# Weight tensors of an FFN copied once to bf16 in HBM, their loads moved to the Sync queue, and a preparation step moved within its slot

## The chip, the cores and the metric

The kernel runs on all 8 cores of one Trainium2 chip. Each core works on its own 2048 tokens, with its own copy of the weights, and no core talks to another. The metric is the device time of the slowest core in microseconds (us). The median of 3 runs of the kernel before is 6087.93 us.

## What is computed

One "sandwich" block on x of shape (4, 4096, 2048), f32 (`_layernorm` has no gain or bias):

```python
def attn(x, Wqkv, bqkv, Wout, bout):          # C=32 groups of K=64
    xc = x.reshape(N, Ls, 32, 64)
    qkv = einsum('nlck,cki->nlci', xc, Wqkv) + bqkv
    q, k, v = split(qkv, 3, axis=-1)
    scores = einsum('nlcd,nled->nldce', q, k) / 8
    attn = softmax(scores, axis=-1)
    ctx = einsum('nldcm,nlcd->nldm', attn, v).transpose(0, 1, 3, 2)
    return einsum('nlck,ko->nlco', ctx, Wout) + bout

def ffn(x, w_gate, w_up, w_down):              # 2048 -> 8192 -> 2048
    gated = silu(x @ w_gate.T) * (x @ w_up.T)
    return gated @ w_down.T

x = x + layernorm(attn(layernorm(x)))
x = x + layernorm(ffn(layernorm(x)))
```

The attention is within one token, between its 32 groups; it is done by elementwise work, not by matmuls. The FFN is the matmul work.

## The kernel before

Features lie on the partitions, tokens on the free axis. **Chunks**: a core's 2048 tokens are 16 chunks of T = 128 tokens for the attention. **Windows**: 4 windows of W = 512 tokens (4 chunks each) for the FFN. The three FFN weights (`wgH`, `wuH`, `wdH`, each 8192 x 2048 in f32, 67 MB) do not fit on the chip, so they are streamed from HBM once for each window, 768 loads in all, and each load casts a block of 128 x 2048 from f32 to bf16 on its way. Such a cast DMA is issued from GpSimd (POOL).

**Slots.** The main loop (L570) runs c from -1 to 16; one turn is a slot. Slot c does: the end of the attention of chunk c-1 (output projection L612, LayerNorm, residual, the new x2, L651, its statistics, and the store of x2 to the HBM scratch `x2h`, "spill", L677, from Sync); if chunk c-1 was the last of its window, `emit_xn2prep` (L528), which reads x2 of the whole window back in 16 DMAs on Sync and normalizes it into `xn2_sb` in 32 vector instructions (L558, L561); the load `dma_xb(c+2)` (L161); the input statistics of chunk c+1 (ACT L694, PE L171); then the attention loop of chunk c, 17 steps j; then `xn1` and QKV of chunk c+1 (L239, L273).

**A step j** (L758): `emit_s(j)`, the score product on the vector engine (L716, 128 x 4096); `emit_z(j-1)`, a tree sum (L725 to L735); `emit_rz` on ACT (L742, L745); `emit_uP(j-1)`, (L302, L311, L320); one `pull(1)`; `emit_exp(j)` on ACT (L753, 3.6 us); another `pull(1)`.

**Atoms.** `pull` emits the next atom of the FFN of the window before: per window 32 `gu` atoms, 16 `down`, 32 `gu`, 16 `down`, `ln4`, `bc4` and 16 `fin`, 114 in all, split over the four slots of the next window at 29 a slot. So slots 0 to 3 have no FFN atoms, slot 4 has 29 `gu` atoms, slots 4 to 15 carry windows 0 to 2, and slot 16 carries window 3 alone. What is left of a slot's atoms after the loop is emitted at its end (after QKV).

- `gu(h)` (L327): loads `wg_sb[h%2]` and `wu_sb[h%2]`, 16 matmuls 128x512 for gate (L341), 16 for up (L351), then three ACT and two vector instructions for silu and product into `gated_sb`.
- `down(hh, dt)` (L384): two halves; each loads `wd_sb[half]` (L391) and runs 16 matmuls (L402) into `dps[dt%2]`. The evacuation is on ACT for hh = 0 (L414) and on the vector engine for hh = 1 (L418).
- `fin(k)` (L496): reads x2 back (`x2s_sb`, Sync), three vector instructions, stores `yT` (Sync).

**Order.** `plan.op` appends to one list per engine ("T" PE, "V" vector, "A" ACT, "G" POOL, "S" Sync), and each engine works its list in the order of emission; a wait of one entry holds all that follow on that engine. A weight load is emitted just before its matmuls and waits only until PE has finished with its buffer two loads earlier. On the POOL list stand `wqkv`, `wout`, three `xb` loads at the start, and then, in order, `xb` and weight loads; `dma_xb(c+2)` waits for the x2 of chunk c-1.

Of the kernel before, what the change touches and what calls it, by code (L numbers as in the profile page):

```python
# [6 lines left out]
BF16 = mybir.dt.bfloat16  # L7
# [4 lines left out]
D = 2048  # L12
HID = 8192
# [38 lines left out]
def build_program(max_slot=NC):  # L52
# [9 lines left out]
    bk_d = nc.dram_tensor("bk", [128, 32], F32, kind="ExternalInput").ap()  # L62
    bv_d = nc.dram_tensor("bv", [128, 16], F32, kind="ExternalInput").ap()
    bo_d = nc.dram_tensor("bo", [128, 1], F32, kind="ExternalInput").ap()
    x2h = nc.dram_tensor("x2h", [D, TOK], BF16, kind="ExternalOutput" if DBG_X2 else "Internal").ap()
    yT = nc.dram_tensor("yT", [D, TOK], F32, kind="ExternalOutput").ap()

# [63 lines left out]
    def dep(*keys):  # L131
        return [last.get(k) for k in keys]
# [24 lines left out]
    def dma_xb(c):  # L157
        buf = xb_sb[c % 3]

        def fn(g, c=c, buf=buf):  # L160
            return g.dma_start(out=buf.ap(),  # L161
                               in_=xH[c * 128:(c + 1) * 128, :])
        last[f"xb{c}"] = plan.op("G", fn, deps=dep(f"x2_{c - 3}"),
                                 inc=f"Dxb{c % 3}")
# [162 lines left out]
    def emit_gu(w, h):  # L327
        pb = h % 2
        def d_g(g, h=h, pb=pb):
            return g.dma_start(out=wg_sb[pb].ap(),  # L330
                               in_=wgT[h * 128:(h + 1) * 128, :])
        tg = plan.op("G", d_g, deps=dep(f"wgfree{pb}"), inc=f"Dwg{pb}")
        def d_u(g, h=h, pb=pb):
            return g.dma_start(out=wu_sb[pb].ap(),
                               in_=wuT[h * 128:(h + 1) * 128, :])
        tu_d = plan.op("G", d_u, deps=dep(f"wufree{pb}"), inc=f"Dwu{pb}")
        first = [tg, last[f"xn2_{w}"]] + dep(f"gufree{pb}")
        tk = None
        for ft in range(NFT):
            def fn(tn, ft=ft, pb=pb):  # L340
                return tn.matmul(out=gps[pb].ap(),  # L341
                                 lhsT=wg_sb[pb].ap()[:, ft * 128:(ft + 1) * 128],
                                 rhs=xn2_sb.ap()[:, ft * W:(ft + 1) * W],
                                 start=(ft == 0), stop=(ft == NFT - 1))
            tk = plan.op("T", fn, deps=first if ft == 0 else (),
                         inc="T" if ft == NFT - 1 else None)
        tgate = tk
        last[f"wgfree{pb}"] = tgate
        for ft in range(NFT):
            def fn(tn, ft=ft, pb=pb):  # L350
                return tn.matmul(out=ups[pb].ap(),  # L351
                                 lhsT=wu_sb[pb].ap()[:, ft * 128:(ft + 1) * 128],
                                 rhs=xn2_sb.ap()[:, ft * W:(ft + 1) * W],
                                 start=(ft == 0), stop=(ft == NFT - 1))
            tk = plan.op("T", fn, deps=[tu_d] if ft == 0 else (),
                         inc="T" if ft == NFT - 1 else None)
        tup = tk
        last[f"wufree{pb}"] = tup
        if h == NHT - 1:
            last["xn2_free"] = tup  # L360
        ta = plan.op("A", lambda a, pb=pb: a.activation(  # L361
            out=e1_sb.ap(), in_=gps[pb].ap(), func=AF.Exp, scale=-1.0),
            deps=[tgate] + dep("e1free"), inc="A")
        ta = plan.op("A", lambda a: a.activation(
            out=e1_sb.ap(), in_=e1_sb.ap(), func=AF.Ln, bias=1.0),
            deps=[ta] + dep("consts"), inc="A")
        ta = plan.op("A", lambda a, pb=pb: a.activation(  # L367
            out=m_sb[pb].ap(), in_=e1_sb.ap(), func=AF.Exp, scale=-1.0),
            deps=[ta] + dep(f"mfree{pb}"), inc="A")
        last["e1free"] = ta  # L370
        tv = plan.op("V", lambda v, pb=pb: v.tensor_mul(  # L371
            out=t1_sb[pb].ap(), in0=m_sb[pb].ap(), in1=gps[pb].ap()),
            deps=[ta, tgate] + dep(f"t1free{pb}"), inc="V")
        last[f"mfree{pb}"] = tv
        hs = h % 32
        tv = plan.op("V", lambda v, hs=hs, pb=pb: v.tensor_mul(  # L376
            out=gated_sb.ap()[:, hs * W:(hs + 1) * W],
            in0=t1_sb[pb].ap(), in1=ups[pb].ap()),
            deps=[tup, tv] + dep(f"gatedfree{hs}"), inc="V")
        last[f"t1free{pb}"] = tv  # L380
        last[f"gufree{pb}"] = tv
        last[f"gated{hs}"] = tv

    def emit_down(w, hh, dt):  # L384
        pb = dt % 2
        tk = None
        for half in (0, 1):
            wb = (2 * dt + half) % 2
            def d_w(g, hh=hh, dt=dt, half=half, wb=wb):
                r0 = (((2 * hh + half) * 16 + dt)) * 128  # L390
                return g.dma_start(out=wd_sb[wb].ap(),  # L391
                                   in_=wdT[r0:r0 + 128, :])
            td = plan.op("G", d_w, deps=dep(f"wdfree{wb}"),
                         inc=f"Dwd{wb}")
            first = [td]
            if half == 0:
                first += [last.get(f"dfree{pb}")] + \
                    [last[f"gated{i}"] for i in range(32)]
            for sh in range(16):
                ht = 16 * half + sh  # L400
                def fn(tn, ht=ht, sh=sh, pb=pb, wb=wb, half=half):
                    return tn.matmul(  # L402
                        out=dps[pb].ap(),
                        lhsT=wd_sb[wb].ap()[:, sh * 128:(sh + 1) * 128],
                        rhs=gated_sb.ap()[:, ht * W:(ht + 1) * W],
                        start=(ht == 0), stop=(ht == 31))
                tk = plan.op("T", fn, deps=first if sh == 0 else (),
                             inc="T" if (sh == 15) else None)
            last[f"wdfree{wb}"] = tk
# [156 lines left out]
    dma_xb(0)  # L566
    dma_xb(1)
    dma_xb(2)

    for c in range(-1, min(max_slot, NC) + 1):  # L570
        pw = (c // CPW) - 1 if 0 <= c < NC else (NW - 1 if c == NC else -1)
# [109 lines left out]
            if cp % CPW == CPW - 1:  # L681
                last[f"spill_w{cp // CPW}"] = ts

        if 0 <= c - 1 < NC and (c - 1) % CPW == CPW - 1:
            emit_xn2prep((c - 1) // CPW)

        if 3 <= c + 2 < NC:
            dma_xb(c + 2)
# [14 lines left out]
        if 0 <= c < NC:  # L703
# [47 lines left out]
            def emit_exp(j):  # L751
# [3 lines left out]
                    deps=[last[f"s_{c}_{j}"]], inc="A")  # L755
                last[f"exp_{c}_{j}"] = ta

            for j in range(NJ + 1):  # L758
                if j < NJ:
                    emit_s(j)  # L760
                if j >= 1:
                    emit_z(j - 1)
                    emit_rz(j - 1)
                if j >= 1:
                    emit_uP(c, j - 1)
                pull(1)
                if j < NJ:
                    emit_exp(j)
                pull(1)

        if 0 <= c + 1 < NC:
            cn = c + 1
# [16 lines left out]
            if "qkv" not in DBG_SKIP:  # L789
# [6 lines left out]

    sems = {name: nc.alloc_semaphore(f"s{name}") for name in plan.counts}

    qsems = {"G": ("Dcq", "Dco", "Dxb0", "Dxb1", "Dxb2",
                   "Dwg0", "Dwg1", "Dwu0", "Dwu1", "Dwd0", "Dwd1"),  # L800
             "S": ("Db", "Dxw", "Dr0", "Dr1", "Do",
                   "Dxr0", "Dxr1", "Dxr2", "Dxr3")}

    def run_stream(eng_handle, name):
        hw = {k: 0 for k in sems}
# [134 lines left out]
```

How the kernel before makes its waits and increments, by code:

```python
    def run_stream(eng_handle, name):  # L804
        hw = {k: 0 for k in sems}
        for fn, waits, inc in plan.ops[name]:
            for s, v in waits:
                if v > hw[s]:
                    eng_handle.wait_ge(sems[s], v)
                    hw[s] = v
            inst = fn(eng_handle)
            if inc is not None:
                inst.then_inc(sems[inc], 16 if inc.startswith("D") else 1)
        for s in qsems.get(name, ()):
            v = plan.counts.get(s, 0)
            if v > hw.get(s, 0):
                eng_handle.wait_ge(sems[s], v)
                hw[s] = v
        return hw
# [18 lines left out]
        @block.sync  # L838
        def _(sync):
            hw = run_stream(sync, "S")
            if out_final and hw.get("Do", 0) < out_final:
                sync.wait_ge(sems["Do"], out_final)
```

## Time and profile before

| what | value |
|---|---|
| timed runs | 6038.36, 6087.93, 6142.63 us; median 6087.93 us |
| the profiled execution | 5889.32 us; span of its slowest core 5887.8 us |
| spans of the 8 cores | 5833.5 to 5887.8 us, granted TensorE clock 0.775 to 0.782 |
| busy share of the span: PE, vector (DVE), ACT, POOL | 56%, 55%, 35%, 7% |
| HBM read, written by the core | 843 MB, 25 MB |
| cast queue (POOL's DMAs) | 413 MB written on chip, 42.4% of the 16 DMA engines' time |
| chain that ended last, by engine | PE 38%, DVE 25%, DMA 15%, issue 11%, ACT 10% |
| the same by line, the first | gate matmuls 13%, up matmuls 12%, load of `wd_sb` 11%, down matmuls 10% |

The profile is of one execution, of the core that took longest. Its times count from the first instruction. "Busy" of PE counts matmuls as modelled; the granted clock is the share of full speed that PE was allowed. A releaser ("<-") is what ended an engine's idle time. The span is some 0.05% shorter than the execution's own time, and the execution is 3.3% shorter than the median of the timed runs.

### The profile page before, as it was taken

To read this page: it belongs to the slowest core of one execution; us is meant where nothing else is said; L and a number is where in the kernel's file an instruction comes from. 1 tells how busy PE (TensorE), PEld (TensorE's weight loads), DVE (VectorE), ACT (ScalarE), POOL (GpSimd) and SP (SyncE) were. 2 spreads that over 40 slices of the span, in tenths; PEclk is the share of its full clock that TensorE was granted. 3 is DMA by queue.
4 is the path that set the end of the run, shared out by engine and by line. 5 is a ranking of instruction groups with operands and counts; after the bars stand their busy time and mean duration, and the time that the engine had idled before them with its cause. 6 is when DMAs were issued, how large, how long until landed. Compare 5 with 4: busy or idle time off the path is not lost.

```text
span 5887.8 us, 47487 instructions; the slowest of 8 cores (5833.5 to 5887.8 us)
## 1 busy us (share of the span) xinstructions
PE 3298.7 (56%) x15536; PEld 1508.5 (26%) x15536; DVE 3220.9 (55%) x3680; ACT 2043.1 (35%) x2953; POOL 415.7 (7%) x790
## 2 busy tenths in 40 slices
PE   1101102967787511967878521867868521988973
PEld 0101001432343201433333201333333200433431
DVE  5686775754656465764656455765557456100102
ACT  3434433442453323452343323452343322211200
POOL 0000000100010000100101000101101000111100
PEclk9955555979889755878978765988979765999996
DMA  1000002845565312745656311745746321977852
GB/s 26 8 0 7 0 7 42 138 73 95 97 116 99 69 32 49 129 73 96 110 95 113 63 41 45 127 75 101 129 73 114 61 55 43 152 118 120 153 100 67
DMA packets 174676, 458.26 MB, mean 78 GB/s; under 512 B 49376, under 2 KB 65760, under 8 KB 174304
## 3 DMA queue, kind: packets, MB, share of 16 engines
q0 software_dynamic: 113184, 413.22, 42.4%
q1 hardware_dynamic: 61248, 41.99, 2.6%
q8 instruction: 128, 2.10, 0.1%
q14 instruction: 116, 0.95, 0.1%
HBM read 843.15 MB, written 25.17 MB: 147 GB/s over the span
## 4 chain that ended last, share of the span: by engine, by line
PE 38%; DVE 25%; DMA 15%; issue 11%; ACT 10%; DVEq 1%; SPq 0%; ACTq 0%; POOL 0%; POOLq 0%
PE gps L341 13%; PE ups L351 12%; DMA wd_sb<-wdH 11%; PE dps L402 10%; DVE es_sb L311 6%; DVE zs_sb L731 4%; DVE ctx_sb L320 3%; DVE zs_sb L725 3%; DVE es_sb L716 3%; ACT kd_sb L252 2%; DMA x2s_sb<-x2h 2%; PE mps L179 1%; ACT v_sb L289 1%; DMA xn_sb<-x2h 1%; ACT q_sb L289 1%
## 5 line engine op out<-in xcount | busy, mean ns | idle before, releaser
L402 PE MATMUL dps<-gated_sb,wd_sb 128*128 128x512 bf16 x4096 | 1011.4, 408 | 376.2 <-DMA wd_sb<-wdH 343.3
L341 PE MATMUL gps<-xn_sb,wg_sb 128*128 128x512 bf16 x4096 | 981.3, 395 | 55.8 <-DVE gated_sb L376 39.7
L351 PE MATMUL ups<-xn_sb,wu_sb 128*128 128x512 bf16 x4096 | 957.5, 388 | 0.0
L753 ACT ACTIVATE es_sb<-es_sb 128x4096 bf16<-128x4096 bf16 x256 | 922.0, 3602 | 11.4 <-DVE es_sb L716 11.4
L239 PE MATMUL mps<-xn_sb,wqkv_sb 128*128 128x128 bf16 x512 | 72.4, 302 | 1426.6 <-DVE xn_sb L784 1375.1
L742 ACT ACTIVATE rz_sb<-zf_sb 128x128 bf16<-128x128 bf16 x256 | 79.0, 308 | 1977.3 <-DVE zf_sb L735 1977.3
L402 PEld LDWEIGHTS dps<-gated_sb,wd_sb 128*128 128x128 bf16 x4096 | 412.0, 103 | 974.9 <-issue 592.0
L311 DVE TENSOR_TENSOR es_sb<-es_sb,u_sb 128x4096 bf16<-128x4096 bf16 x256 | 586.8, 2292 | 27.7 <-DVE u_sb L302 1.4
L716 DVE TENSOR_TENSOR es_sb<-q_sb,kd_sb 128x4096 bf16<-128x4096 bf16 x256 | 584.7, 2285 | 8.7 <-DVE ctx_sb L316 0.5
L371 DVE TENSOR_TENSOR t_sb<-m_sb,gps 128x512 bf16<-128x512 bf16 x256 | 175.2, 685 | 719.4 <-ACT m_sb L367 718.3
L320 DVE TENSOR_TENSOR ctx_sb<-ctx_sb,es_sb 128x4096 bf16<-128x4096 bf16 x240 | 550.0, 2292 | 26.0 <-DVE es_sb L311 1.4
L341 PEld LDWEIGHTS gps<-xn_sb,wg_sb 128*128 128x128 bf16 x4096 | 409.9, 101 | 590.7 <-issue 215.1
L351 PEld LDWEIGHTS ups<-xn_sb,wu_sb 128*128 128x128 bf16 x4096 | 408.1, 100 | 507.4 <-issue 102.0
L239 PEld LDWEIGHTS mps<-xn_sb,wqkv_sb 128*128 128x128 bf16 x512 | 45.9, 129 | 1456.6 <-issue 1456.6
L731 DVE TENSOR_TENSOR zs_sb<-zs_sb 128x1024 bf16<-128x1024 bf16 (+2 forms) x768 | 360.8, 470 | 81.3 <-DVE zs_sb L731 1.8
L725 DVE TENSOR_TENSOR zs_sb<-es_sb 128x2048 bf16<-128x2048 bf16 x256 | 311.9, 1218 | 134.4 <-ACT es_sb L753 134.4
L192 DVE TENSOR_SCALAR st_sb<-mps 1x128 f32<-1x128 f32 x48 | 13.4, 279 | 518.6 <-PE mps L179 518.6
L361 ACT ACTIVATE e_sb<-gps 128x512 f32<-128x512 f32 x256 | 149.7, 585 | 382.2 <-PE gps L341 382.2
L418 DVE TENSOR_TENSOR y_sb<-y_sb,dps 128x512 bf16<-128x512 bf16 x64 | 43.8, 685 | 376.9 <-PE dps L402 376.7
L302 DVE TENSOR_TENSOR u_sb<-v_sb,rz_sb 128x128 bf16<-128x128 bf16 x256 | 57.7, 225 | 324.2 <-ACT rz_sb L745 324.2
L414 ACT ACTIVATE y_sb<-dps 128x512 bf16<-128x512 f32 x64 | 38.2, 597 | 560.6 <-PE dps L402 560.6
L391 POOL DMA_DIRECT2D wd_sb<-wdH x256 | 135.7, 531 | 1349.4 <-PE dps L402 1303.8
(84 smaller groups left out, 2376.0 us busy)
## 6 DMA issues: line engine op xcount, KB each, us to landing
wg_sb<-wgH POOLq DMA_DIRECT2D x256, 512.0 KB, 6.5
wu_sb<-wuH POOLq DMA_DIRECT2D x256, 512.0 KB, 6.6
wd_sb<-wdH POOLq DMA_DIRECT2D x256, 512.0 KB, 5.5
yT<-outs_sb SPq DMA_DIRECT2D x64, 256.0 KB, 2.5
xb_sb<-xH POOLq DMA_DIRECT2D x16, 512.0 KB, 9.1
x2h<-x2c_sb SPq DMA_DIRECT2D x16, 512.0 KB, 4.3
xn_sb<-x2h SPq DMA_DIRECT2D x64, 128.0 KB, 2.7
x2s_sb<-x2h SPq DMA_DIRECT2D x64, 128.0 KB, 3.4
```

Source lines behind the costliest of these rows:

```text
L311: tp = plan.op("V", lambda v, s3=s3, ub=ub: v.tensor_tensor(out=s3, in0=s3, in1=ub, op=ALU.mult), deps=[tu], inc="V")
L320: tg = plan.op(eng, lambda g, buf=buf: g.tensor_add(out=ctx_sb.ap(), in0=ctx_sb.ap(), in1=buf.ap()), deps=[tp, last[f"ctxadd_{c}_{j - 1}"] ...
L341: return tn.matmul(out=gps[pb].ap(), lhsT=wg_sb[pb].ap()[:, ft * 128:(ft + 1) * 128], rhs=xn2_sb.ap()[:, ft * W:(ft + 1) * W], start=(ft = ...
L351: return tn.matmul(out=ups[pb].ap(), lhsT=wu_sb[pb].ap()[:, ft * 128:(ft + 1) * 128], rhs=xn2_sb.ap()[:, ft * W:(ft + 1) * W], start=(ft = ...
L361: ta = plan.op("A", lambda a, pb=pb: a.activation(out=e1_sb.ap(), in_=gps[pb].ap(), func=AF.Exp, scale=-1.0), deps=[tgate] + dep("e1free") ...
L371: tv = plan.op("V", lambda v, pb=pb: v.tensor_mul(out=t1_sb[pb].ap(), in0=m_sb[pb].ap(), in1=gps[pb].ap()), deps=[ta, tgate] + dep(f"t1fre ...
L391: return g.dma_start(out=wd_sb[wb].ap(), in_=wdT[r0:r0 + 128, :])
L402: return tn.matmul(out=dps[pb].ap(), lhsT=wd_sb[wb].ap()[:, sh * 128:(sh + 1) * 128], rhs=gated_sb.ap()[:, ht * W:(ht + 1) * W], start=(ht ...
L716: v.tensor_tensor(out=s3, in0=qb, in1=k3, op=ALU.mult), deps=d, inc="V")
L725: tz = plan.op("V", lambda v, buf=buf: v.tensor_add(out=zs_sb.ap(), in0=buf.ap()[:, 0:16 * T], in1=buf.ap()[:, 16 * T:32 * T]), deps=[last ...
L731: tz = plan.op("V", lambda v, ww=ww: v.tensor_add(out=zs_sb.ap()[:, 0:ww], in0=zs_sb.ap()[:, 0:ww], in1=zs_sb.ap()[:, ww:2 * ww]), deps=[t ...
L753: ta = plan.op("A", lambda a, buf=buf: a.activation(out=buf.ap(), in_=buf.ap(), func=AF.Exp, scale=0.125), deps=[last[f"s_{c}_{j}"]], inc="A")
```

## The change

Three HBM tensors `wgc`, `wuc`, `wdc` in bf16 are added. At the start, after the three `xb` loads, twelve DMAs on POOL copy and cast the weights into them, in quarters of 2048 rows, in the order g0, u0, d0, g1, u1, d1, and so on. All 768 weight loads of the atoms now read the bf16 copies, are issued from Sync instead of POOL, and wait for the quarter they read (`wcg`, `wcu`, `wcd`) besides their buffer. So `dma_xb(3)` and later ones follow the twelve copies on POOL, and the weight loads share Sync's list with spills, read-backs and `yT` stores.

In slots 4, 8 and 12 `emit_xn2prep` is emitted after step j = 4 of the attention loop instead of before the loop, and in every first slot of a window `pull` is called only from j = 5 on. In slot 16 it stays where it was.

```diff
--- before.py
+++ after.py
@@ -62,6 +62,9 @@
     bk_d = nc.dram_tensor("bk", [128, 32], F32, kind="ExternalInput").ap()
     bv_d = nc.dram_tensor("bv", [128, 16], F32, kind="ExternalInput").ap()
     bo_d = nc.dram_tensor("bo", [128, 1], F32, kind="ExternalInput").ap()
+    wgc = nc.dram_tensor("wgc", [HID, D], BF16, kind="Internal").ap()
+    wuc = nc.dram_tensor("wuc", [HID, D], BF16, kind="Internal").ap()
+    wdc = nc.dram_tensor("wdc", [HID, D], BF16, kind="Internal").ap()
     x2h = nc.dram_tensor("x2h", [D, TOK], BF16, kind="ExternalOutput" if DBG_X2 else "Internal").ap()
     yT = nc.dram_tensor("yT", [D, TOK], F32, kind="ExternalOutput").ap()
 
@@ -328,12 +331,14 @@
         pb = h % 2
         def d_g(g, h=h, pb=pb):
             return g.dma_start(out=wg_sb[pb].ap(),
-                               in_=wgT[h * 128:(h + 1) * 128, :])
-        tg = plan.op("G", d_g, deps=dep(f"wgfree{pb}"), inc=f"Dwg{pb}")
+                               in_=wgc[h * 128:(h + 1) * 128, :])
+        tg = plan.op("S", d_g, deps=dep(f"wgfree{pb}", f"wcg{h // 16}"),
+                     inc=f"Dwg{pb}")
         def d_u(g, h=h, pb=pb):
             return g.dma_start(out=wu_sb[pb].ap(),
-                               in_=wuT[h * 128:(h + 1) * 128, :])
-        tu_d = plan.op("G", d_u, deps=dep(f"wufree{pb}"), inc=f"Dwu{pb}")
+                               in_=wuc[h * 128:(h + 1) * 128, :])
+        tu_d = plan.op("S", d_u, deps=dep(f"wufree{pb}", f"wcu{h // 16}"),
+                       inc=f"Dwu{pb}")
         first = [tg, last[f"xn2_{w}"]] + dep(f"gufree{pb}")
         tk = None
         for ft in range(NFT):
@@ -389,8 +394,9 @@
             def d_w(g, hh=hh, dt=dt, half=half, wb=wb):
                 r0 = (((2 * hh + half) * 16 + dt)) * 128
                 return g.dma_start(out=wd_sb[wb].ap(),
-                                   in_=wdT[r0:r0 + 128, :])
-            td = plan.op("G", d_w, deps=dep(f"wdfree{wb}"),
+                                   in_=wdc[r0:r0 + 128, :])
+            td = plan.op("S", d_w,
+                         deps=dep(f"wdfree{wb}", f"wcd{2 * hh + half}"),
                          inc=f"Dwd{wb}")
             first = [td]
             if half == 0:
@@ -566,6 +572,13 @@
     dma_xb(0)
     dma_xb(1)
     dma_xb(2)
+    for s in range(4):
+        for name_, dst_, src_ in (("g", wgc, wgT), ("u", wuc, wuT),
+                                  ("d", wdc, wdT)):
+            def fcache(g, dst_=dst_, src_=src_, s=s):
+                return g.dma_start(out=dst_[s * 2048:(s + 1) * 2048, :],
+                                   in_=src_[s * 2048:(s + 1) * 2048, :])
+            last[f"wc{name_}{s}"] = plan.op("G", fcache, inc=f"Dwc{name_}{s}")
 
     for c in range(-1, min(max_slot, NC) + 1):
         pw = (c // CPW) - 1 if 0 <= c < NC else (NW - 1 if c == NC else -1)
@@ -681,8 +694,11 @@
             if cp % CPW == CPW - 1:
                 last[f"spill_w{cp // CPW}"] = ts
 
-        if 0 <= c - 1 < NC and (c - 1) % CPW == CPW - 1:
-            emit_xn2prep((c - 1) // CPW)
+        def xn2prep_if_due():
+            if 0 <= c - 1 < NC and (c - 1) % CPW == CPW - 1:
+                emit_xn2prep((c - 1) // CPW)
+        if not (0 <= c < NC):
+            xn2prep_if_due()
 
         if 3 <= c + 2 < NC:
             dma_xb(c + 2)
@@ -755,6 +771,7 @@
                     deps=[last[f"s_{c}_{j}"]], inc="A")
                 last[f"exp_{c}_{j}"] = ta
 
+            jp0 = 5 if c % CPW == 0 else 0
             for j in range(NJ + 1):
                 if j < NJ:
                     emit_s(j)
@@ -763,10 +780,14 @@
                     emit_rz(j - 1)
                 if j >= 1:
                     emit_uP(c, j - 1)
-                pull(1)
+                if j >= jp0:
+                    pull(1)
                 if j < NJ:
                     emit_exp(j)
-                pull(1)
+                if j >= jp0:
+                    pull(1)
+                if j == 4:
+                    xn2prep_if_due()
 
         if 0 <= c + 1 < NC:
             cn = c + 1
@@ -796,10 +817,11 @@
 
     sems = {name: nc.alloc_semaphore(f"s{name}") for name in plan.counts}
 
-    qsems = {"G": ("Dcq", "Dco", "Dxb0", "Dxb1", "Dxb2",
-                   "Dwg0", "Dwg1", "Dwu0", "Dwu1", "Dwd0", "Dwd1"),
+    qsems = {"G": tuple(["Dcq", "Dco", "Dxb0", "Dxb1", "Dxb2"]
+                        + [f"Dwc{n}{s}" for n in "gud" for s in range(4)]),
              "S": ("Db", "Dxw", "Dr0", "Dr1", "Do",
-                   "Dxr0", "Dxr1", "Dxr2", "Dxr3")}
+                   "Dxr0", "Dxr1", "Dxr2", "Dxr3",
+                   "Dwg0", "Dwg1", "Dwu0", "Dwu1", "Dwd0", "Dwd1")}
 
     def run_stream(eng_handle, name):
         hw = {k: 0 for k in sems}
```

## Rows read from the trace of the kernel before

**Rows 1.** The page, 40 slices of 147 us: busy tenths of PE.

```profile
PE   1101102967787511967878521867868521988973
```

**Rows 2.** Groups by line: count, busy us, mean ns, idle us before, what ended it.

```profile
L402 PE MATMUL dps<-gated_sb,wd_sb 128*128 128x512 bf16 x4096 | 1011.4, 408 | 376.2 <-DMA wd_sb<-wdH 343.3 <-DVE gated_sb L376 28.2 <-DVE ctx_sb L320 2.2
L341 PE MATMUL gps<-xn_sb,wg_sb 128*128 128x512 bf16 x4096 | 981.3, 395 | 55.8 <-DVE gated_sb L376 39.7 <-DVE xn_sb L561 15.0 <-DMA wg_sb<-wgH 1.0
```

**Rows 3.** Timeline in the down stretch of slot 5: start us, duration, engine, line.

```profile
1470.24 0.53 POOL L391 DMA_DIRECT2D wd_sb<-wdH  x1 [3.58 <-PE dps L402]
...
1471.77 3.61 PE L402 MATMUL dps<-gated_sb,wd_sb 128*128 128x512 bf16 x16 [2.07 <-DMA wd_sb<-wdH]
...
1480.02 0.53 POOL L391 DMA_DIRECT2D wd_sb<-wdH  x1 [3.57 <-PE dps L402]
```

**Rows 4.** Windows: length, busy us (count) per engine, clock, DMA share, GB/s.

```profile
1312.00:1658.00 346.00, 240.38 (x1122) 108.43 (x1122) 185.40 (x201) 124.98 (x182) 31.15 (x59) 0.86 0.55 92
1340.00:1510.00 170.00, 120.66 (x511) 50.00 (x512) 82.38 (x76) 40.62 (x39) 17.94 (x34) 0.95 0.57 98
...
5015.00:5218.00 203.00, 201.99 (x937) 91.43 (x936) 41.13 (x60) 53.82 (x87) 30.08 (x57) 1.00 0.97 150
5218.00:5391.00 173.00, 124.55 (x513) 50.77 (x512) 0.00 (x0) 9.24 (x16) 17.95 (x34) 0.93 0.59 99
5391.00:5612.00 221.00, 220.63 (x1023) 99.81 (x1020) 43.50 (x64) 59.71 (x97) 32.71 (x62) 1.00 0.88 151
```

**Rows 5.** Timeline, vector engine: the score product, once per step j, three places.

```profile
595.95 2.29 DVE L716 TENSOR_TENSOR es_sb<-q_sb,kd_sb 128x4096 bf16<-128x4096 bf16 x1
...
607.45 2.29 DVE L716 TENSOR_TENSOR es_sb<-q_sb,kd_sb 128x4096 bf16<-128x4096 bf16 x1
...
1110.15 2.28 DVE L716 TENSOR_TENSOR es_sb<-q_sb,kd_sb 128x4096 bf16<-128x4096 bf16 x1
...
1125.35 2.28 DVE L716 TENSOR_TENSOR es_sb<-q_sb,kd_sb 128x4096 bf16<-128x4096 bf16 x1
...
1425.23 2.29 DVE L716 TENSOR_TENSOR es_sb<-q_sb,kd_sb 128x4096 bf16<-128x4096 bf16 x1
...
1445.58 2.29 DVE L716 TENSOR_TENSOR es_sb<-q_sb,kd_sb 128x4096 bf16<-128x4096 bf16 x1
```

**Rows 6.** The page's DMA issues: line, queue, count, KB each, median us to landing.

```profile
wd_sb<-wdH POOLq DMA_DIRECT2D x256, 512.0 KB, 5.5
yT<-outs_sb SPq DMA_DIRECT2D x64, 256.0 KB, 2.5
...
x2h<-x2c_sb SPq DMA_DIRECT2D x16, 512.0 KB, 4.3
...
wqkv_sb<-wqkv POOLq DMA_DIRECT2D x1, 2048.0 KB, 18.8
```

**Rows 7.** The page's DMA queues: packets, MB, share of 16 engines' span.

```profile
q0 software_dynamic: 113184, 413.22, 42.4%
```

**Rows 8.** Timeline at the start of slot 2.

```profile
511.93 0.37 SPq L677 DMA_DIRECT2D x2h<-x2c_sb  x1
...
512.40 0.53 POOL L161 DMA_DIRECT2D xb_sb<-xH  x1 [231.47 <-DVE x2c_sb L651]
...
515.57 1.06 PE L171 MATMUL mps<-xb_sb,ones_c 128*1 128x128 bf16 x16
...
524.11 4.47 DVE L716 TENSOR_TENSOR es_sb<-q_sb,kd_sb 128x4096 bf16<-128x4096 bf16 x2
```

**Rows 9.** DMA issues of the first 60 us.

```profile
xb_sb<-xH POOLq DMA_DIRECT2D x3, 512.0 KB, 23.9
```

**Rows 10.** Timeline at the start of slot 4.

```profile
977.09 0.53 POOL L161 DMA_DIRECT2D xb_sb<-xH  x1 [232.54 <-DVE x2c_sb L651]
...
1001.31 0.42 DVE L558 TENSOR_TENSOR xn_sb<-xn_sb,a2bc_sb 128x512 bf16<-128x512 bf16 x1 [1.13 <-DMA xn_sb<-x2h]
...
1015.03 2.27 DVE L716 TENSOR_TENSOR es_sb<-q_sb,kd_sb 128x4096 bf16<-128x4096 bf16 x1
```

## The prediction

> **What bounds the kernel now.** I read the page's slices first [rows 1]. Up to slice 6 PE is nearly idle: slots 0 to 3 have attention and no FFN work. Then FFN and attention share the core (slots 4 to 15), and the last six slices or so are FFN alone. Next the groups by line [rows 2], for what ended PE's idle time: it stood 343.3 us before L402, the down matmuls, for `wd_sb`, while the gate matmuls waited 1.0 us for their weights (39.7 us went to `gated_sb`). So two buffers suffice for gate and up, and not for down.
>
> The windows and the timeline show how. At 1470 us [rows 3] a half of a down atom needs 3.61 us of PE and has waited 2.07 us; its load is issued when PE has read the buffer two halves back, and lands some 5.5 us later [rows 6]. Issue to issue of one buffer is 1470.24 to 1480.02, 9.8 us for the two halves of one `dt`. PE could do them in 7.2 us. A down `dt` took 170/16 = 10.6 us in slot 5 and 173/16 = 10.8 us in the last window [rows 4]. The granted clock of these stretches (0.93 to 0.95, a mean of both levels) is below the 1.00 of the gate/up stretch at 5391 us, where PE never waits: the gaps cost clock also.
>
> Elsewhere PE is not the limit. One step j of a slot takes 11.5 us without FFN work (595.95 to 607.45 us), 15.2 us with two gate/up atoms, and 20 to 21 us with two down atoms of the first half [rows 5]. In the first two the vector engine sets the pace; in the third it waits, in the end for PE. Only the third can shrink by faster loads, and its floor is two atoms of PE, 14.4 us.
>
> **The change, part by part.**
>
> *(a) Faster down loads: gain.* All 768 weight loads move to SP and read bf16, half the bytes. No load of this kind is in the trace. The old one takes 5.5 us. The mean packet of the cast queue took 0.424 x 5887.8 x 16 / 113184 = 0.353 us, eight per DMA engine and load, so 2.8 us is transfer and 2.7 us is fixed; with half the bytes read I estimate 1.4 us plus a fixed part as SP's rows have it. Bounds on SP: 256 KB in 2 KB rows lands in 2.5 us, 512 KB in small pieces in 4.3 us [rows 6, 7]. I take 3.4 us, since 4 KB rows resemble the first more. Now 9.8 us is 5.5 us of landing and 4.3 us of PE and handover; SP also starts sooner, since after the same vector instruction SP issued at 511.93 and POOL at 512.40 [rows 8], 0.4 to 0.5 us. That makes 3.4 + 4.3 - 0.4 = 7.3 us per `dt`; with some slow clock 7.5. Gain: 96 `dt` in slots x (10.7 - 7.5) = 307 us (10.7 for the slots where down and other atoms alternate) and 32 at the end x (10.8 - 7.5) = 106 us, together about 410 us. At 4.3 us landing a `dt` costs 8.2 to 8.6 us and the gain is some 290 us; at PE's own pace (7.2 us) it is 336 + 115 = 451 us. Gate and up loads waited for nothing and bring nothing.
>
> *(b) The caches: cost.* Twelve DMAs on POOL read 12 x 16.8 = 201 MB as f32 and write 101 MB as bf16, HBM to HBM. They stand in the queue behind `wqkv` and the first three `xb` loads (landed by about 28 us) [rows 9] and **ahead of `dma_xb(3)`**. All of the cast DMAs of the trace ran on one queue, q0 [rows 7], so I expect `xb3` to come only after the last cache byte. What waits: at slot 2's start PE's L171 reads `xb3` at 515.57, and ACT's L694 soon after [rows 8]. Both engines take work in order; behind them stand the exp of the softmax and, through the statistics, the vector engine's first L716. Nothing covers this: slots 0 to 3 have no FFN work. The stall is (end of the cache + some 7 us for `xb3`) - 516 us. The end:
> - quickest: 24576 rows of 4 KB at the mean packet time, 24576 x 0.353 / 16 = 542 us, end at 570, stall 61 us;
> - at the pace of the `wqkv` load, the only large one (2048 KB written, 4.19 MB read, 18.8 us [rows 6]): 201.3 / 4.19 x 18.8 = 903 us, end at 931, stall 422 us;
> - slowest: in 5015 to 5218 us the core wrote 150 GB/s into SBUF, so read 300 GB/s from HBM, with the DMA engines 0.97 busy, against 0.88 for the same rate at 5391 us [rows 4]: memory already slows packets. If that is the limit for reads and writes together, 302 MB take 1007 us, stall 526 us.
>
> I take 421 us. The quickest would need 302 / 542 = 557 GB/s of HBM traffic per core, nearly twice anything in the trace, so the truth is nearer to the other two.
>
> The Trainium skill ("HBM Reference", Specifications) gives about 716 GB/s per stack, shared by the two cores on it. By that figure, an estimate, the caches take 2 x 302 MB / 716 GB/s = 843 us and the stall is about 362 us; no run so far shows HBM-to-HBM traffic.
>
> The first cached weights are needed in slot 4 (1015 us before, later now), so the SP waits on `wcg0` and the others are over by then, even in the slowest case with its stall.
>
> *(c) `xn2` preparation moved behind j = 4 in slots 4, 8, 12: about nothing.* Before, the vector engine waits at the boundary to slot 4 for the read-backs of x2. From the issue of the `xb` load to the slot's first L716 it is 11.7 us in slot 2 (512.40 to 524.11) [rows 8] and 37.9 us in slot 4 (977.09 to 1015.03) [rows 10], so 26 us are exposed. After: the reads land during steps 0 to 4; the vector work stays, 32 x 0.42 us [rows 10] = 13.4 us. So 12.6 us are saved. But steps 0 to 4 have no atoms, the remaining 12 steps hold 24, and five of the 29 gate/up atoms come after QKV with the vector engine all but idle: 5 x 6.9 (221 us for 32 atoms) [rows 4] = 35 us. Against this, a step with two atoms costs 3.7 us more than one without: 14.5 such steps before, 12 after, so 9 us less. Sum per window: -12.6 + 35 - 9 = +13; where the five atoms overlap ACT's evacuations it is less: I take +7 us each, +20 in all, bounds 0 and +50.
>
> *(d) SP's queue.* Weight loads now stand behind the spill (waits for x2), the read-backs and the `yT` stores (wait for the vector engine). Before, they stood behind `dma_xb(c+2)`, which waits for the same x2 [rows 8]; in fin phases no weights are wanted. Nothing. Where a weight load was late at a slot start (all gate matmuls together waited 1.0 us) [rows 2], nothing either.
>
> **Sum** against the profiled span: 5887.8 - 410 + 421 + 20 = 5919 us, 0.5% up. The profiled execution took 5889.32 us and the timed runs 6087.93 us in the median, 3.4% more. Scaled: 6088 x 1.0053 = 6120 us. In slower executions PE is slower, so (a) may give less there.
>
> **Rivals.**
> 1. *The caches run at the DMA engines' pace* (stall 61 us). For: the packet time of the queue as a mean. Against: the traffic it needs. Span 5887.8 - 410 + 61 + 20 = 5559 us, about 5748 us. A `xb3` that overtakes the caches would end near there as well (another 60 us less). It decides from a stall under about 270 us, caches done by 780 us.
> 2. *Other side: HBM takes reads and writes at 300 GB/s per core together* (stall 526 us). Span 6024 us, 2.3% up, about 6229 us. For: the busy share of 0.97. Against: that rate was what PE asked for, not proven a ceiling. It decides from a stall of about 510 us, that is caches ending after 1020 us.
> 3. *SP's loads land in 4.3 us*: gain 290 us, span 6039 us, about 6244 us. For: the only 512 KB row on SP. Against: its pieces are small.
> 4. *The clock*: once waits are gone, PE may be granted no more than the mean 0.86 of slot 5 [rows 4]; a `dt` then costs 7.2 / 0.86 = 8.4 us, the gain is 96 x 2.3 + 32 x 2.4 = 298 us, the span 6031 us, about 6236 us.
>
> **Chances.** My forecast (stall 300 to 510, gain near 410): 0.50. Rival 1 with overtaking: 0.19. Rival 2: 0.16. Rivals 3 and 4: 0.15. The forecast's own range is 6000 to 6215 us. A comparison of this kernel can tell about 2% (122 us) from no change: faster 0.20 (rival 1 and the forecast's lower edge), same 0.50, slower 0.30 (rivals 2 to 4, nearly whole). Range for 8 in 10: it leaves out rival 1 (0.19), reaches to 6260 us for rivals 2 to 4, and 5960 us below, a stall of some 265 us.
>
> **What would show it.** The vector and PE slices should be empty from about 516 to 930 us, with ACT's L694 waiting for `xb_sb` near 420 us, and DMA full from 28 us on. `PE dps L402 <- DMA wd_sb` should fall from 343 us to under 60 us, `wd_sb` land in about 3.4 us from SP, and steps with two down atoms take 15 us. Slot 4 should lose its wait for `xn_sb<-x2h` and show five gate/up atoms behind QKV. I am wrong if `xb3` lands before 800 us, or if down steps stay above 17 us.

## The result, and the profile after

The changed kernel takes 6002.4 us in the median of its runs, the kernel before 6022.25 us over all runs made beside it. The ratio is **1.0119, 95% interval 1.0083 to 1.0155**: by 2% no difference, but reliably above 1. Executions in which one die had a lower granted clock are in the medians and not in the ratio, which is why the two stand in another order. I forecast 1.0053 (6120 us, range 5960 to 6260) and 0.50 for "same". The two profiled spans are 5887.8 and 5989.8 us, +102 us. The ratio is worth only some 70 us: the profiled execution of the kernel before (5889 us) was quicker than all ten timed beside the changed one (5909 us at best), so differences of spans against 5888 us, here and below, are up to some 30 us too large.

The page of the changed kernel: busy tenths in 40 slices of 150 us, the rate of the DMA engines, and the two queues.

```profile
PE   1101000101979686315886866039796960399993
...
DVE  5681004686846585668556664768365856520112
...
DMA  9999994001434232112332422114242320244442
GB/s 116 109 109 109 109 109 51 7 0 35 135 91 148 77 127 78 48 36 100 113 120 92 131 81 74 39 56 139 90 151 74 127 75 31 85 151 144 150 136 79
...
q1 hardware_dynamic: 171840, 444.69, 22.8%
q0 software_dynamic: 5856, 111.18, 16.6%
```

Against [rows 1] there is a hole: PE and the vector engine are all but idle from about 0.5 to 0.95 ms, while the DMA engines are full and write 109 GB/s. After it, DMA is half as busy as before for the same work. The waits of the changed kernel (engine, line, what it waited for: us in total, times, longest):

```profile
DVE x2c_sb L664 <- DMA x2h<-x2c_sb: 368.8, 1, 368.8
...
PE mps L174 <- DMA xb_sb<-xH: 104.2, 2, 79.4
...
ACT sq_sb L710 <- DMA xb_sb<-xH: 77.4, 1, 77.4
...
PE dps L408 <- DMA wd_sb<-wdc: 51.7, 67, 4.0
```

The last answers to [rows 2]: 343.3 us have become 51.7. The first two are the price, 368.8 + 79.4 us in one place. The prediction's sign, ACT waiting near 420 us for `xb_sb`, is not there: that wait is 77.4 us. Here it is in time (L664 computes the x2 of a chunk, L690 issues the spill, L164 the `xb` load, L732 is the score product; compare [rows 8]):

```profile
280.16 0.38 SPq L690 DMA_DIRECT2D x2h<-x2c_sb  x1
...
878.98 1.23 DVE L664 TENSOR_TENSOR x2c_sb<-xb_sb,sq_sb 128x2048 bf16<-128x2048 bf16 x1 [368.85 <-DMA x2h<-x2c_sb]
...
963.30 1.86 PE L174 MATMUL mps<-xb_sb,ones_c 128*1 128x128 bf16 x16 [79.37 <-DMA xb_sb<-xH]
...
969.82 4.47 DVE L732 TENSOR_TENSOR es_sb<-q_sb,kd_sb 128x4096 bf16<-128x4096 bf16 x2
```

The spill of chunk 0 is issued at 280 us and lands at 879: 600 us instead of the usual 4.3. The vector engine needs `x2c_sb` free for the next chunk, so it stands still from 510 to 879 us, before `xb3` matters at all; `xb3` then adds 79 us. The stretch of the copies as a window, and the two that answer to 1340 and 5218 us in [rows 4] (the first with a few gate and up matmuls at its start):

```profile
39.00:971.00 932.00, 57.63 (x473) 41.38 (x473) 338.37 (x352) 204.65 (x315) 1.08 (x2) 0.63 0.99 109
1776.00:1914.00 138.00, 126.16 (x547) 53.54 (x558) 90.89 (x85) 45.56 (x47) 0.00 (x0) 0.97 0.41 135
5418.00:5540.00 122.00, 113.81 (x506) 48.81 (x517) 0.51 (x1) 9.50 (x16) 0.00 (x0) 1.00 0.45 147
```

The score products of steps with two down atoms in the changed kernel; these two steps take 14.2 and 15.1 us, the 42 steps of the trace with down atoms alone take 14 to 18 us, 15.4 in the mean, against 21.4 before ([rows 5] has one of 20.4):

```profile
1823.30 2.29 DVE L732 TENSOR_TENSOR es_sb<-q_sb,kd_sb 128x4096 bf16<-128x4096 bf16 x1
...
1837.46 2.29 DVE L732 TENSOR_TENSOR es_sb<-q_sb,kd_sb 128x4096 bf16<-128x4096 bf16 x1
...
1852.52 2.29 DVE L732 TENSOR_TENSOR es_sb<-q_sb,kd_sb 128x4096 bf16<-128x4096 bf16 x1
```

Its page's DMA issues (size, median time from issue to landing) have the load at 3.4 us, against 5.5 in [rows 6]:

```profile
wd_sb<-wdc SPq DMA_DIRECT2D x256, 512.0 KB, 3.4
wgc<-wgH POOLq DMA_DIRECT2D x4, 8192.0 KB, 448.9
```

The clearest view is the length of each slot (e1 to e9 are the experiments below; e5 and e10 are not in it), worked out from the trace as the time from the first score product of a slot to that of the next (us; the last column is slot 15 and 16 to the end of the span):

```
slot      1    2    3    4    5    6    7    8    9   10   11   12   13   14  15-16   span
before  232  232  259  297  346  318  380  298   351  318  371  298  346  309  1241   5888
after   678  231  233  328  301  297  335  326   301  298   333  328  298  290  1121   5990
e1      665  232  260  295  338  310  382  296   353  320   384  295   356  309  1223   6308
e2      232  232  233  327  352  318  362  327   346  309   355  325   357  315  1244   5922
e3      593  231  233  325  300  299  333  326   298  297   334   325  304  292  1122   5904
e4      717  232  233  327  302  293  338  325   297  297   334   325  299  292  1114   6015
e6      231  245  233  325  299  300  339  325   300  297   334   325  302  293  1122   5562
e7      232  232  233  327  301  297  336  326   300  298   333   325  301  290  1121   5544
e8      232  232  302  295  300  295  349  296   300  298   348  295   300  292  1124   5548
e9      232  232  233  327  301  297  349  296   300  298   348  296   299  291  1159   5550
```

Slot 1 grows by 446 us. The eleven down stretches together shrink from 1355 to 974 us, 381 us less (128 `dt`, 10.6 to 7.6 us each). Slots 3 and 4 together grow by 5 us. What is left, about 32 us, is 7 us in slots 7 and 8 together, 10 in slots 11 and 12, 11 in slots 15 and 16, and the rest in between: +446 - 381 + 5 + 32 = 102.

### The profile page after: what moved, and what is told of

Its sections match the earlier page's. It is cut to its first block, busy times and chain, and to the rows that moved or that the text cites. A ratio compares the mean times of both kernels' runs of the same rounds, so it can differ in the third digit from the quotient of the medians.

```text
span 5989.8 us, 47305 instructions; the slowest of 8 cores (5971.8 to 5989.8 us)
## 1 busy us (share of the span) xinstructions
PE 3134.8 (52%) x15282; PEld 1468.4 (25%) x15536; DVE 3222.2 (54%) x3680; ACT 2043.7 (34%) x2953; POOL 16.4 (0%) x34
## 4 chain that ended last, share of the span: by engine, by line
PE 34%; DVE 28%; issue 12%; ACT 10%; another core or an unknown queue 7%; DMA 7%; DVEq 1%; SPq 0%; ACTq 0%; POOL 0%; POOLq 0%
PE gps L346 11%; PE dps L408 11%; PE ups L356 9%; DVE es_sb L314 6%; DMA wd_sb<-wdc 4%; DVE zs_sb L747 4%; DVE ctx_sb L323 4%; DVE es_sb L732 4%; DVE zs_sb L741 3%; ACT kd_sb L255 2%; DMA x2s_sb<-x2h 2%; PE mps L182 1%; ACT q_sb L292 1%; ACT v_sb L292 1%
## 5 line engine op out<-in xcount | busy, mean ns | idle before, releaser
L346 PE MATMUL gps<-xn_sb,wg_sb 128*128 128x512 bf16 x4008 | 943.7, 387 | 282.9 <-DVE xn_sb L567 200.5
L408 PE MATMUL dps<-gated_sb,wd_sb 128*128 128x512 bf16 x4013 | 918.4, 383 | 92.8 <-DMA wd_sb<-wdc 51.7
L356 PE MATMUL ups<-xn_sb,wu_sb 128*128 128x512 bf16 x4013 | 923.1, 380 | 4.5
L732 DVE TENSOR_TENSOR es_sb<-q_sb,kd_sb 128x4096 bf16<-128x4096 bf16 x256 | 584.7, 2286 | 9.6 <-DVE ctx_sb L319 0.5
L408 PEld LDWEIGHTS dps<-gated_sb,wd_sb 128*128 128x128 bf16 x4096 | 390.8, 98 | 619.7 <-issue 194.2
L356 PEld LDWEIGHTS ups<-xn_sb,wu_sb 128*128 128x128 bf16 x4096 | 401.5, 98 | 485.8 <-issue 10.6
L174 PE MATMUL mps<-x2c_sb,ones_c 128*1 128x128 bf16 x256 | 29.8, 309 | 443.3 <-DVE x2c_sb L664 443.3
L664 DVE TENSOR_TENSOR x2c_sb<-xb_sb,sq_sb 128x2048 bf16<-128x2048 bf16 x16 | 19.6, 1226 | 370.8 <-DMA x2h<-x2c_sb 368.8
L381 DVE TENSOR_TENSOR gated_sb<-t_sb,ups 128x512 bf16<-128x512 bf16 x256 | 176.1, 688 | 76.2 <-PE ups L356 59.2
```

The source lines that it names most:

```text
L346: return tn.matmul(out=gps[pb].ap(), lhsT=wg_sb[pb].ap()[:, ft * 128:(ft + 1) * 128], rhs=xn2_sb.ap()[:, ft * W:(ft + 1) * W], start=(ft = ...
L356: return tn.matmul(out=ups[pb].ap(), lhsT=wu_sb[pb].ap()[:, ft * 128:(ft + 1) * 128], rhs=xn2_sb.ap()[:, ft * W:(ft + 1) * W], start=(ft = ...
L381: tv = plan.op("V", lambda v, hs=hs, pb=pb: v.tensor_mul(out=gated_sb.ap()[:, hs * W:(hs + 1) * W], in0=t1_sb[pb].ap(), in1=ups[pb].ap()), ...
L408: return tn.matmul(out=dps[pb].ap(), lhsT=wd_sb[wb].ap()[:, sh * 128:(sh + 1) * 128], rhs=gated_sb.ap()[:, ht * W:(ht + 1) * W], start=(ht ...
L732: v.tensor_tensor(out=s3, in0=qb, in1=k3, op=ALU.mult), deps=d, inc="V")
```

## The experiments

### One part alone: the copies, the move

**e1** adds only the copies to the kernel before, at the same place:

```diff
     dma_xb(2)
+    for s in range(4):
+        for name_, dst_, src_ in (("g", wgc, wgT), ("u", wuc, wuT),
+                                  ("d", wdc, wdT)):
+            def fcache(g, dst_=dst_, src_=src_, s=s):
+                return g.dma_start(out=dst_[s * 2048:(s + 1) * 2048, :],
+                                   in_=src_[s * 2048:(s + 1) * 2048, :])
+            last[f"wc{name_}{s}"] = plan.op("G", fcache, inc=f"Dwc{name_}{s}")
```

> The kernel before, with only the twelve copies added at the same place on POOL; the f32 loads and the place of the xn2 preparation stay. Nobody reads the copies. Theory (the change's cost is all in the copies, and they cost one stall in slot 2): slot 1 grows by about 446 us as in the changed kernel, nothing else moves, the span is 5888 + 446 = 6334 us. Rival (the copies also cost the later loads, or the stall needs the SP traffic of the changed kernel): slot 1 grows by clearly less or more than 446 us, or slots 4 to 15 change by more than 10 us together.

Measured: span 6308 us, slot 1 665 us (+433), and the same two waits:

```profile
DVE x2c_sb L661 <- DMA x2h<-x2c_sb: 360.2, 1, 360.2
...
PE mps L174 <- DMA xb_sb<-xH: 98.7, 2, 74.8
```

So the theory holds: the stall does not need the new loads. It is 13 us shorter than in the changed kernel, as the copies end 13 us sooner (947 us against 960). Slots 4 to 14 sum to 3638 us, against 3632 before. Slots 15 and 16 are 18 us shorter; with f32 loads they scatter as much from core to core (1218 to 1257 us on three cores of e10 below).

**e2** makes only the move (the changed kernel's `xn2prep_if_due`, `jp0` and the call behind j = 4; no copies, f32 loads on POOL).

> The kernel before, with only the xn2 preparation moved behind j = 4 and atoms from j = 5 on in slots 4, 8 and 12; no copies, f32 loads on POOL. Theory (the move trades a wait of 26 us for five exposed gate/up atoms): slot 3 loses 26 us, slot 4 gains about 31 us, in sum +5 to +10 us a window, the span +20 us, 5908 us. Rival (the move pays, its cost came from the bf16 loads): span below 5888 us.

Measured: span 5922 us, of its slowest core. Slots 3 and 4: 559 us against 556; 7 and 8: 688 against 678; 11 and 12: 680 against 668. The wait at the boundary goes (slot 3 is 26 us shorter) and slot 4 is 29 us longer. So +3 to +12 us a window, with the scatter of the f32 down stretches in slots 7 and 11 in it; over the means of all eight cores it is +4, +3 and +8 us. The theory (+5 to +10) holds in the main, and the rival (the move pays) does not.

### Why slot 2 waits: which transfer is the gate

**e3** loads chunk 3 of x ahead of the copies, into `gated_sb[:, 0:2048]` (the lines that redirect its readers there are left out):

```diff
     dma_xb(2)
+    dma_xb(3)
     for s in range(4):
...
-        if 3 <= c + 2 < NC:
+        if 4 <= c + 2 < NC:
```

> The changed kernel, but the input chunk 3 is loaded ahead of the twelve copies (into a part of gated_sb that is free until slot 4). Theory A, of the prediction (slot 2 waits because xb3 stands behind the copies in q0, and for nothing else): the stall of 446 us is gone, the span about 5545 us. Theory B (the store of x2 of chunk 0 to HBM gets one small packet through between two copy packets of 4.8 us, so it takes 128 x 4.7 = 600 us; it holds x2c_sb and is a second gate nearly as late): the vector engine still waits for the spill until about 879 us, the stall shrinks by no more than the 79 us that came after it, the span about 5910 us.

Measured: span 5904 us, 86 us less than the changed kernel. The wait on `xb3` is gone, the other one stands:

```profile
DVE x2c_sb L668 <- DMA x2h<-x2c_sb: 361.1, 1, 361.1
```

Theory A, the only reason that the prediction gives, is refuted as the sole cause: with `xb3` in time, four fifths of the stall remain.

**e4** takes `xb3` back behind the copies and makes these of small rows:

```diff
-            def fcache(g, dst_=dst_, src_=src_, s=s):
-                return g.dma_start(out=dst_[s * 2048:(s + 1) * 2048, :],
-                                   in_=src_[s * 2048:(s + 1) * 2048, :])
...
+            for hc in range(2):
+                def fcache(g, dst_=dst_, src_=src_, s=s, hc=hc):
+                    return g.dma_start(
+                        out=dst_[s * 2048:(s + 1) * 2048,
+                                 hc * 1024:(hc + 1) * 1024],
+                        in_=src_[s * 2048:(s + 1) * 2048,
+                                 hc * 1024:(hc + 1) * 1024])
...
```

> The changed kernel, but each copy is made in two column halves, so that a contiguous piece is 4 KB read and 2 KB written instead of 64 KB and 32 KB. Theory B (one small packet of the spill per copy packet): the spill of chunk 0 lands in under 100 us instead of 600. If HBM bounds the copies (302 MB at 327 GB/s): they end near 965 us still, xb3 is as late as before, the stall stays near 446 us, the span near 5990 us. If the large packets themselves bound them (64 KB in 4.8 us is 13.6 GB/s an engine, against 25 GB/s for the 4 KB packets of the weight loads): the copies end at 550 to 650 us, the stall is 40 to 140 us, the span 5590 to 5690 us.

Measured: span 6015 us. The spill of chunk 0 lands in 60 us, and nothing waits for it; the whole stall is now `xb3`. The scalar engine's longest wait for it:

```profile
ACT sq_sb L715 <- DMA xb_sb<-xH: 484.3, 1, 484.3
```

The slices of its page:

```profile
DMA  9999995001334242102333322114242321244442
GB/s 108 102 106 109 109 109 66 0 7 35 107 104 133 77 141 67 66 28 91 120 113 111 116 95 71 41 42 140 93 150 73 126 82 33 77 153 138 157 140 81
```

Two things follow. The spill's 600 us came from the size of the copies' packets: 2048 pieces of 256 bytes are 128 for each DMA engine, and 600 / 128 = 4.7 us is the time of one copy packet, since 3072 packets of 32 KB (64 KB read) on 16 engines took 932 us, 4.85 us each. One small packet of q1 passes for each large one of q0. The changed kernel's queues between 300 and 500 us, while the spill is under way, have it directly (packets, MB, share of 16 engines):

```profile
q0 software_dynamic: 715, 21.86, 100.2%
q1 hardware_dynamic: 715, 0.18, 0.7%
```

The Trainium skill ("DMA: Bandwidth & Descriptors", Queues, rings and completion order) states that each DMA engine goes round its queues by packets and changes only at a packet's end; the trace agrees, with 4.7 against 4.85 us, and shows what that means when one queue's packets are 128 times as large. And the copies are not bound by large packets: small ones are no faster (some 970 us instead of 932).

e3 and e4 together: spill and `xb3` are two gates, one behind the other. Opening one alone gains 86 us (e3) or loses 25 (e4, with its slower copies).

### What bounds the copies

**e10** replaces the copies by 192 f32 loads that read the same 201 MB into `gated_sb` and write nothing to HBM (each waits for the load eight before it):

```diff
+    for i in range(192):
+        src_ = (wgT, wuT, wdT)[i // 16 % 3]
...
+            return g.dma_start(
+                out=gated_sb.ap()[:, i % 8 * 2048:(i % 8 + 1) * 2048],
+                in_=src_[r0:r0 + 128, :])
+        last[f"rd{i % 8}"] = plan.op("G", fread, deps=dep(f"rd{i % 8}"),
+                                     inc=f"Drd{i % 8}")
```

> The kernel before, and in place of the copies 192 f32 loads of 128 x 2048 from the same weight tensors, cast to bf16 into eight regions of gated_sb, eight in flight, ahead of xb3 on POOL; nobody uses what they load. It reads the same 201 MB as the twelve copies and writes nothing to HBM. If HBM's total traffic bounds the copies (302 MB in 925 us is 327 GB/s a core): reading alone takes 201 / 327 = 616 us or less, down to 542 us at the mean packet time of before; xb3 arrives by 580 to 660 us, the stall is 70 to 150 us, the span 5960 to 6040 us. If reading f32 at 218 GB/s is itself the bound: the reads end at 965 us, the stall is 446 us, the span 6330 us.

Measured: slot 1 is 349 us, a stall of 117 us, span 6016 us. The page's slices:

```profile
DMA  9999100573647331573747320754747321967952
GB/s 165 171 170 170 33 7 0 98 126 63 108 75 133 58 61 36 105 119 70 119 78 125 58 55 28 129 95 86 121 74 119 62 55 41 151 113 120 153 96 68
```

Four full slices at 165 to 171 GB/s into SBUF, so some 340 GB/s read, against 218 GB/s read and 109 GB/s written by the copies, 327 GB/s together. Reading f32 is not the bound (218 became 340), and the total of HBM traffic is nearly the same in both. The simplest reading of the two is that the traffic itself sets the copies' time, at about 330 to 340 GB/s a core with all cores at it. That is argued from two equal totals: no run wrote to HBM alone or left cores idle, so a separate limit of the writes is not excluded. The Trainium skill ("HBM Reference", Specifications) gives about 358 GB/s a core when both cores of a stack stream; the runs stay 5 to 9% under it.

### What the loads gain: bytes or queue

**e5** is e7 (below) with the bf16 loads issued from POOL instead of SP:

```diff
-        tg = plan.op("S", d_g, ...
+        tg = plan.op("G", d_g, ...
```
(and the same for `tu_d` and `td`)

> As e7, but the bf16 weight loads are issued from POOL as the f32 loads were; it tells apart what half the bytes bring and what the queue brings. If it is the bytes (transfer 2.8 to 1.4 us of 5.5 us): landing 4.1 us, a down dt 8.2 to 8.5 us, steps with two down atoms about 17 us, the span 80 to 120 us above e7. If the queue brings nothing: landing near 3.5 us and the span as e7. If the queue brings it all: landing 5.5 us, steps of 20 us, the span some 380 us above e7.

Measured on cores 4 to 7, whose granted clock (0.795 to 0.797) was like e7's (0.789 to 0.794): spans 5604 to 5624 us, against 5528 to 5544 us of the same cores in e7, some 77 us more. That is just under the 80 to 120 us expected if the bytes do it. The landing of its down load, on core 6:

```profile
wd_sb<-wdc POOLq DMA_DIRECT2D x256, 512.0 KB, 3.7
```

Two score products of the same core, a step with two down atoms between them:

```profile
1375.70 2.29 DVE L741 TENSOR_TENSOR es_sb<-q_sb,kd_sb 128x4096 bf16<-128x4096 bf16 x1
...
1391.67 2.29 DVE L741 TENSOR_TENSOR es_sb<-q_sb,kd_sb 128x4096 bf16<-128x4096 bf16 x1
```

A down `dt` takes 1061/128 = 8.3 us here, 10.6 before, 7.6 from SP. Of the 3.0 us gained per `dt`, 2.3 come with the bf16 source and 0.7 with the queue. The landing differs by 0.2 to 0.3 us (3.7 and 3.4 us). The rest is POOL's later start: after the last matmul of a half, where PE then waits for `wd_sb`, the next load's issue begins 0.54 us later on POOL (before and e5) and 0.08 us later on SP (after and e7), a difference of 0.46 us, as [rows 8] has it.

### Keeping the gain without the stall

**e6** spreads the copies: quarter 0 at the start, quarters 1 to 3 behind the `xb` load of slots 1 to 3.

```diff
+    copy_quarter(0)
...
             dma_xb(c + 2)
+            if 1 <= c <= 3:
+                copy_quarter(c)
```

> The changed kernel with the twelve copies spread: the quarter 0 at the start, the quarters 1, 2 and 3 issued in slots 1, 2 and 3, each right behind that slot's xb load. Large packets as in the changed kernel. Three copies take 925 / 4 = 231 us, a slot without FFN work 232 us. Theory B (a spill passes one small packet per copy packet): xb waits for nothing, but the spill issued at a slot's start is held until that slot's copies drain, 231 to 240 us later, and then needs a few us more, so the next slot's x2 (L664) waits some 5 to 15 us each time; the stall is 15 to 40 us in all instead of 446, the span 5560 to 5590 us. Theory A alone (only xb behind the copies matters): no stall, 5545 us.

Measured: span 5562 us. Of the stall one wait is left, as theory B has it, once instead of three times. The spill issued at 512 us, when the slot before still had a copy in flight (to 521 us), landed at 754 us; the next two were issued after the copies had drained or nearly so and landed in 4 and 11 us:

```profile
DVE x2c_sb L666 <- DMA x2h<-x2c_sb: 13.0, 1, 13.0
```

**e7** is e6 with the small rows of e4. The expectation calls e6 the interleaved kernel.

> As the interleaved kernel, and each copy made in column halves, 2 KB written per piece. Theory B: the spills land at once and the remaining stall of the interleaved kernel goes too; the copies take 243 us a slot (973 / 4) and lag a slot by some 11 us each, which nothing in slots 0 to 3 notices, since xb is wanted a slot later. Span about 5545 us, ratio to the kernel before 0.94. Rival (the HBM traffic of the copies slows something else, or the first cached weights are late in slot 4): span above 5600 us.

Measured: **ratio 0.9384 (0.9359 to 0.9410)**, span 5544 us. No wait on spill or `xb3`, though three of the four spills beside the copies still take 41 to 55 us; the hole is gone and the copies (105 GB/s) run beside the attention:

```profile
DVE  5686866774658567683658567683658567210112
...
DMA  9999999643423210242423221242424221444442
```

**e8** is e7 with the preparation back at the slot's start, as before the change.

> As e7, and the xn2 preparation is back at the slot's start with atoms from j = 0, as in the kernel before. Theory (the move costs 5 to 8 us a window, as seen alone): 15 to 25 us faster than e7, span about 5525 us. Rival (with fast loads on SP the read-backs are no longer slowed by weight loads of the POOL queue, so the old place is cheaper than it was): more than 30 us faster. Other rival (SP's read-backs now hold back the weight loads): slower than e7.

Measured: ratio 0.9387 (0.9367 to 0.9406), span 5548 us: no better than e7, against my main expectation. The table shows why. Slots 7 + 8 and 11 + 12 are 17 and 15 us shorter than in e7, but slots 3 + 4 are 37 us longer (14 to 37 us over the eight cores), and one wait stands there:

```profile
DVE xn_sb L564 <- DMA xn_sb<-x2h: 59.3, 13, 44.1
```

What it waits for first is not the read-backs but the spill of chunk 3, which they must follow: issued at 976 us beside the last copies, it lands at 1021 us, 45 us later instead of 4 to 6, and only then does SP issue the first read-back:

```profile
976.16 0.36 SPq L697 DMA_DIRECT2D x2h<-x2c_sb  x1
1021.28 26.91 SPq L554 DMA_DIRECT2D xn_sb<-x2h  x16
```

The read-backs themselves take 5 to 10 us each there, against 2 to 6 in slot 8. The expectation of e9 below puts the whole wait on them; its cost of the place stands all the same.

**e9** therefore moves the preparation in slot 4 only.

> As e7 (interleaved copies in small pieces, loads on SP), but the xn2 preparation is moved only in slot 4 and stands at the slot's start in slots 8 and 12. From e8: the old place cost 38 us more than the moved one in slots 3 and 4, where the read-backs stood in the traffic of the last copies (a wait of 44 us), and 16 to 17 us less in each of the two later windows. If those costs are additive: 33 us below e7, span about 5510 us, ratio to the kernel before 0.933. If they were chance: the same as e7, 0.938.

Measured: ratio 0.9366 (0.9325 to 0.9406). Slots 1 to 14 sum to 4099 us against 4131 for e7, near the 33 us expected. The span of its slowest core (5550 us) is not below e7's: its slots 15 and 16 took 1159 us at a granted clock of 0.80, against 1121 us at 0.84 in e7. Cores 4 to 7, at e7's clock, have a median span of 5496 us against 5533. So the trace shows the gain, but by the ratios alone e9 and e7 cannot be told apart.

## Why the prediction was right, and where not

The sum said 410 us gained, 421 us lost by a stall, 20 us by the move; measured are 381, 446 and about 38 us for the move and all else. The forecast, about no change and slightly up, held because the two large terms were sized within 10% each. All three errors point the same way, though (29, 25 and 18 us), so +31 us of span was forecast and +102 measured: of the small difference between large terms, the sum had the sign and not the size.

- **(a), down loads: right in mechanism, 29 us too large.** The landing was taken at 3.4 us and is 3.4 us, the `dt` at 7.5 and is 7.6 us, a step at 15 us and is 15.4 in the mean. The 3.4 us was picked between two rows of other loads (2.5 and 4.3 us), so its exactness is luck. The 29 us are about half the new `dt`, 0.1 us more than taken, and half the old one, which I took at 10.7 and 10.8 us from two windows; over all stretches it is 10.6.
- **(b), the time of the copies: right in size, by luck in its source.** Taken at 903 us by the pace of `wqkv`, measured 932. That pace is 223 GB/s read, of one load into SBUF with its start in it; e10 reads the same weights into SBUF at 340 GB/s. So the `wqkv` row measures something else than what held the copies at 218 GB/s, and that the two agree is chance. The reason against the quickest case, the traffic it would need (557 GB/s), fits what e10 shows.
- **(b), what waits: half wrong.** That `xb3` stands behind the copies is so (e4), but I named it as the only gate. The spill was not considered: part (d) went through SP's list only for who waits behind whom in issue, not for how long its own DMAs take beside the copies. The step that failed is "I expect `xb3` to come only after the last cache byte. What waits: ...", as a full list. It did not spoil the number, since the spill's gate opens at 879 us, 84 us before that of `xb3`; that too is luck, as nothing in the prediction saw to it. It would have spoiled the next edit: someone who trusts it makes e3 and gains 86 us of 446.
- **(c), the move: right in size as a change to the kernel before** (e2: +3 to +12 us a window against +7), but its price depends on the rest. The 26 us exposed [rows 10] were in part the four f32 weight loads ahead of the read-backs: those landed at 990 to 1001 us, the four read-backs issued beside them took 10 to 17 us, and those issued after them 2 to 4 us. With bf16 loads on SP, behind the read-backs, 13 to 15 us are exposed at the ends of slots 7 and 11 (e8 against e7), and the move costs 15 to 17 us a window there, while in slots 3 and 4 it saves 37 us beside the last copies.
- **(d), SP's queue: right**, no wait of the trace points to an order on SP. Of the 38 us of "the move and all else", 22 lie at the three boundaries that the move changes (5, 7 and 10 us); the other 16, of which 11 in slots 15 and 16, I cannot assign.
- **Rivals.** 1 (engine pace) is out by the 932 us themselves, and by e4 for small rows. 2 (300 GB/s for reads and writes together) is, as far as e10 goes, the right mechanism with a ceiling of 327. 3 (landing 4.3 us) and 4 (a lower clock) did not occur: the down stretches have clocks of 0.97 and 1.00, above the 0.95 and 0.93 of [rows 4].

## What to carry to other kernels

A one-time copy in a stretch where DMA is idle looks free. Before counting on it, look at every other transfer of that stretch: what stands behind it in its own queue, and what shares the DMA engines from another queue in much smaller pieces. Split such a copy so that each part drains before the next small transfer is needed, issue each part behind the load that must not wait, and keep its contiguous pieces small (here 2 KB instead of 32 KB written): here that turned +1.2% into -6.2%. Nearly all of it came with the spreading (e6); the small pieces brought 18 us more (5562 to 5544 us). When a wait has two gates, removing one shows little; list all of them before judging a fix.

## What the runs showed of the hardware

- A store of 512 KB in 256-byte pieces from SP took 600 us beside a copy with 32 KB packets (one small packet for each large one, 715 and 715 in 200 us), 41 to 60 us beside one with 2 KB packets, at nearly the same DMA load (shares 0.99 and 0.97), and 4.3 us by itself.
- HBM-to-HBM cast copies ran at about 327 GB/s of traffic a core in large packets and 311 in small ones (932 and about 970 us for 302 MB), with all eight cores at it; reads alone reached 340 GB/s.
- A 512 KB load in 4 KB rows lands in 3.4 us from SP and 3.6 to 3.7 us from POOL when it does not cast, against 5.5 us from POOL with an f32 source. After the matmul that frees its buffer, SP began the issue in 0.08 us and POOL in 0.54 us (medians).
